# A row gather in a graph attention kernel gets a bound, and edges outside a slot's block get an index past it

## The reference, cut to what matters

```
q, k, v = feats @ Wq.T + bq, feats @ Wk.T + bk, feats @ Wv.T + bv     # 8 heads of 32
sim  = sum(q[dst] * k[src]) * scale          # per edge and head
attn = softmax of sim over the edges of one dst
agg[dst] += attn * v[src]
x = x + agg @ Wo.T + bo
```

## Time and profile before

| | us |
|---|---|
| median of 3 runs | 6892.29 |
| the profiled execution's own time | 6941.69 |
| its span, first to last instruction | 6939.9 |
| attention loop in it | about 3812 to 6740 |
| gathers `kv<-kvt,sI` (L1249) | 1760 of mean 1.008 |

### The profile page before, as it was taken

How to read it: one execution, slowest core, us unless ns; L and a number is a source line. 1 busy time by engine, 2 the same in 40 slices (tenths; PEclk the granted TensorE clock), 3 DMA queues, 4 the chain that set the end, 5 groups by cost and what they waited for, 6 DMA issues and landing times. The chain is left out here.

```text
span 6939.9 us, 112013 instructions
## 1 busy us (share of the span) xinstructions
PE 4544.0 (65%) x19717; PEld 2978.0 (43%) x16197; DVE 4539.5 (65%) x12295; ACT 3970.3 (57%) x14482; POOL 4648.7 (67%) x3716
## 2 busy tenths in 40 slices
PE   1356666666666666664886677777777777777777
PEld 1244444444444545553553333334333333434335
DVE  4565555555555666663554777777777777777766
ACT  0665555555555555552332577777777767777761
POOL 1478888888888888887554566666666666666630
PEclk6677777777777777776998888888888888888889
DMA  8767777777777777777874566666666666676756
GB/s 303 196 103 107 106 106 105 104 107 106 108 107 106 106 110 108 109 109 167 274 260 136 173 188 192 192 190 195 194 192 195 200 200 197 201 206 201 204 151 194
DMA packets 644159, 1129.71 MB, mean 163 GB/s; under 512 B 74529, under 2 KB 466795, under 8 KB 643445
## 3 DMA queue, kind: packets, MB, share of 16 engines
q0 software_dynamic: 367600, 678.97, 50.2%
q1 hardware_dynamic: 223985, 273.78, 12.1%
q10 hardware_dynamic: 51860, 169.74, 7.3%
HBM read 929.80 MB, written 451.51 MB: 199 GB/s over the span
## 5 line engine op out<-in xcount | busy, mean ns | idle before, releaser
L701 POOL DMA_INDIRECT sums<-mtw,posIw x1563 | 2492.0, 1594 | 599.5 <-issue 404.5
L1249 POOL DMA_INDIRECT kv<-kvt,sI x1760 | 1774.2, 1008 | 1027.4 <-ACT room L1631 596.1
L1631 ACT ACTIVATE room<-kv,pp 128x33 f32<-128x33 f32 x8800 | 1932.3, 308 | 107.2 <-issue 101.8
L734 PE MATMUL ps<-h,wf 128*128 x3320 | 1220.8, 522 | 310.0 <-DVE mtw L825 237.3
L1551 PE MATMUL ps<-room,Of 128*128 128x264 f32 x3520 | 1130.8, 459 | 372.2 <-DVE acc L1734 189.0
L718 PE MATMUL ps<-Mw,Oh 128*128 128x128 f32 x3320 | 672.6, 368 | 918.6 <-DVE Oh L852 918.6
L825 DVE SCALAR_TENSOR_TENSOR mtw<-mtw,cont,ps 128x256 f32 x1660 | 794.1, 478 | 620.2 <-SPq L690 459.9
L718 PEld LDWEIGHTS ps<-Mw,Oh 128*128 128x128 f32 x3320 | 631.7, 274 | 1035.3 <-DVE Oh L852 1004.4
L734 PEld LDWEIGHTS ps<-h,wf 128*128 128x128 f32 x3320 | 816.9, 263 | 590.1 <-issue 451.4
L1551 PEld LDWEIGHTS ps<-room,Of 128*128 128x128 f32 x3520 | 707.6, 219 | 659.6 <-issue 278.6
L799 ACT COPY wf<-ps 128x512 f32<-128x512 f32 x415 | 242.4, 584 | 1234.4 <-PE ps L718 902.9
(11 more groups left out here) (224 smaller groups left out, 4796.5 us busy)
## 6 DMA issues: line engine op xcount, KB each, us to landing
qb<-qt SPq DMA_DIRECT2D x880, 192.0 KB
accd<-acc SPq DMA_DIRECT2D x880, 132.0 KB
ints<-srows ACTq DMA_DIRECT2D x205, 512.0 KB
OT<-drows SPq DMA_DIRECT2D x110, 512.0 KB
sums<-zero ACTq DMA_DIRECT2D x72, 704.0 KB
part<-sums SPq DMA_DIRECT2D x56, 896.0 KB
kv<-kvt,sI POOLq DMA_INDIRECT x1760
kvt<-kvo SPq DMA_DIRECT2D x98, 260.0 KB
```

The source lines that it names most:

```text
L701: e.indirect_dma_start(sums[t % NS], bass.IndirectOffsetOnAxis(ap=posI[:, t % NP:t % NP + 1], axis=0), mt[:, t % NM, :], None, compute_op= ...
L734: m = e.matmul(psum[2 + q % 4][:, j % 2 * D:j % 2 * D + D], lhsT=BT[:, g % 3, j % 4, :], rhs=h[:, bass.ds(own[j % 4], 1), :].rearrange("p ...
L1249: e.indirect_dma_start(kv[:, s % NK, :], None, kvt, bass.IndirectOffsetOnAxis(ap=sI[:, s:s + 1], axis=0)).then_inc(kvs.sem(s), 16)
L1631: e.activation(pv[:, s % NV, h * 33:h * 33 + 33], kv[:, s % NK, D + h * 33:D + h * 33 + 33], ACT.Copy, scale=pp[:, w % 2, h, s % W2:s % W2 ...
```

## The change

`gather` gets a bound, `NB * P - 1` = 12543, the last row of the table, and an index above it is no error: that row is not fetched. In the preparation block DVE works out which edges lie outside their slot's block, `(dl2 - 63.5)² > 4096`, for all slots from the 128th on, and adds 65536 to their index, except on partition 0, whose row is always fetched. The first 128 slots keep their indices, and with them each of the 44 ring buffers is filled once in full; a row that is not fetched leaves there what an earlier slot brought.

```diff
             e.indirect_dma_start(kv[:, s % NK, :], None, kvt, bass.IndirectOffsetOnAxis(
-                ap=sI[:, s:s + 1], axis=0)).then_inc(kvs.sem(s), 16)
+                ap=sI[:, s:s + 1], axis=0), bounds_check=NB * P - 1, oob_is_err=False).then_inc(kvs.sem(s), 16)
...
+            far = sb(stack, "far", [P, R2 - P], BF16)
+            skip = sb(stack, "skip", [P, 1])
...
+                e.memset(skip[:, :], 65536.0).then_inc(S("t_skip"), 1)
+                e.wait_ge(S("t_skip"), 1)
+                e.memset(skip[0:1, :], 0.0).then_inc(S("t_skip"), 1)
                 for c in range(C2):
...
+                e.wait_ge(S("t_column"), 2 * C2)
+                e.tensor_scalar(far[:, :], dl2[:, P:R2], 0.5 - P / 2, None, ALU.add).then_inc(S("t_far"), 1)
+                e.wait_ge(S("t_far"), 1)
+                e.tensor_tensor(far[:, :], far[:, :], far[:, :], ALU.mult).then_inc(S("t_far"), 1)
+                e.wait_ge(S("t_far"), 2)
+                e.tensor_scalar(far[:, :], far[:, :], P * P / 4, None, ALU.is_gt).then_inc(S("t_far"), 1)
+                e.wait_ge(S("t_skip"), 2)
+                e.wait_ge(S("t_far"), 3)
+                e.scalar_tensor_tensor(out=sI[:, P:R2], in0=far[:, :], scalar=skip[:, 0:1], in1=sI[:, P:R2],
+                                       op0=ALU.mult, op1=ALU.add)
```

## The result

The changed kernel takes 6939.9 us (median of four runs, 6933.0 to 6951.5) where the kernel before takes 6893.5 (6885.3 to 6896.2) on the same chip. The ratio is 1.0075 [1.0062, 1.0089], so it is slower by 46 us. The forecast was 6776, faster by 116. The profiled execution of the change is close to its median (6938.8 us, span 6936.9), while that of before lay 49 us above its own. So I compare counts, durations and waits between the two pages, and not their spans.

What follows compares the result with a forecast made beforehand. The loop was taken as bound by waits, long gather runs holding up PE and SP. Rows not fetched -121, bound 0, DVE +4.9: -116 us from 6892.3 gives 6776 us, range 6620 to 7010 (the forecast's own 6640 to 6850).

Steps and rivals of the forecast that it cites:

- A long run of gathers holds up what PE and SP owe to the others: Attention loop: other engines' waits let go 2.3 to 2.5 us after POOL stops; ACT's held-up waits total 457.5 us.
- I take one half: -121 us: Loop gathers: rows not fetched give back 2.5 us at each of 97 crossings, 242 us, of which half arrives.
- first rival: Loop: traffic is not what holds it, so rows not fetched bring nothing; 6897 us, chance 0.19.
- these bytes are of another queue: Loop DMA: argument against the no-change rival, whose 3.77 MB more were hardware-queue traffic, not in the gathers' way.
- four long flushes: Loop, SP: 10.76 us over four flushes during a gather run, held not to agree fully with queues taking turns.
- So no cost: Loop gathers: the bound adds 0 to 0.1 us each, covered by POOL's 5.3 us over per window, 0.33 a gather.
- The rival of the dearer gather: Loop gathers on POOL: the bound lengthens all 1760, deciding from 0.33 us extra; 7150 or 7458 us, chance 0.26.
- DVE's operations, +4.9 us: Preparation block: four added DVE operations and two memsets lie on the path, +4.9 us, bounds +3 to +7.
- The data: Loop: unfetched rows hold another node's k and v, but zero one-hot columns leave sizes and counts the same; no cost.
- The sum: Whole kernel: -121 + 4.9 = -116 us, from a median of 6892.3 to 6776 us.
- if they stay, traffic is not the cause: Loop sign: ACT's waits ahead of `tops` and `lim` should fall from 457.5 to some 340 us.
- the rows are fetched all the same: Sign: queue 0 packets should fall 11% over the loop; if they don't, the rows are still being fetched.

Runs made afterwards that it cites:

- pause_quad: Kernel before plus a POOL memset behind each quad's four gathers, from the twelfth quad on; 6862.1 us, ratio 0.9893, on the chip of 6930 us.
- before: The kernel before, unchanged, in the profile behind the prediction; profiled execution 6941.7 us, median of its timed runs 6893.5.
- skip_all_4: Changed kernel with nearly all rows from the 128th slot on beyond the bound; 6984.6 us, 1.0075 against the kernel before, on the chip of 6935 us.
- bound_only_4: Kernel before with only the bound put on each gather, every row fetched; 6985.7 us, ratio 1.0076, on the chip of 6935 us.
- after_again: The changed kernel, unchanged, timed again beside the kernel before on the chip of 6930 us; 6988.9 us, ratio 1.0084.
- ops_only: Kernel before plus DVE's four operations, no bound, added offset zero; 6350.6 us, ratio 0.9998, on the chip of 6356 us.
- skip_all: Changed kernel with nearly all rows from the 128th slot on beyond the bound; 6527.1 us, 1.0264 against the kernel before, on the chip of 6356 us.
- bound_only: Kernel before with only the bound put on each gather, every row fetched; 6525.5 us, ratio 1.0264, on the chip of 6356 us.
- before_again: The kernel before, unchanged, run for a second profile on the chip of 6356 us; 6350.0 us, ratio 0.9995, span 6343.7.

## Why the prediction was wrong

**"A long run of gathers holds up what PE and SP owe to the others": borne out in part.** `pause_quad` agrees with it by a gain of 68 us against 372.7 us of added work, and in `before`, from 3830 to 6600 us, 80 of ACT's 96 waits over 2 us of this kind end while no gather runs, though gathers fill some six tenths of the loop. The release comes at a median of 1.4 us after the last gather, and not 2.3 to 2.5; the two places that I had read were long ones. It was seen on three chips only: on the three others the same instructions have no such wait.

**"I take one half: -121 us" for rows not fetched: this step failed.** The term is 0. The 2.5 us that I gave back for each crossing went by the quieter queue that missing rows leave, and the hold-up does not hang on what that queue moves: with the share of queue 0 at 2.8% for 55.4% it is the same. What is left is the gathers as such, and an empty one is issued like a full one: as long, and with as many packets. (The working beside it has a slip: 0.77 us of the engines for a gather counts 64 packets. By the earlier trace rows 48.94 MB are 184 gathers, so it is 80 packets and 0.96 us; the forecast took 1.25 and did not use it.) The forecast had this as its first rival, with the right argument in the earlier trace rows (3.77 MB more at no cost), and I gave it 0.19 against 0.47. I set the argument aside because "these bytes are of another queue". With it went what I had cited from the Trainium skill (page "DMA: Bandwidth & Descriptors", section "SWDGE vs HWDGE vs iDMA") on queues taking turns, to which I had opposed four long flushes. `skip_all_4` gives the time that I had drawn from that rule, no change by the rows; that the engines take turns it does not show, since its packets are as many.

**"So no cost" for the bound: this step failed too, and it is what made the sign.** The extra, 0.052 us, is within the 0 to 0.1 that I took. The cover was wrong. I read 26.1 - 20.8 = 5.3 us a window as time that POOL has over, from which an extra of 0.33 us would be paid. (With the mean gather of 1.008 us for the 0.95 it is 4.4 us and 0.28; that does not save the step, for the extra is a fifth of it and was not covered.) As I read it now, that idle time is what a hold-up leaves, at its own moments; between two of them POOL issues back to back, and a longer gather moves all behind it. The runs show how much arrives, not this path. `bound_only_4` has 92 us more of gathers by the medians and is 51 us slower, the first comparison 46, `after_again` 59: about half is absorbed, not all. Where there are no hold-ups nothing is: 182 us of gathers for 170 us of time. The rival of the dearer gather had the right sign and mechanism at a price six times smaller than its threshold; a threshold was the wrong form.

**DVE's operations, +4.9 us: right in size,** 4.2 us in the trace and nothing measurable in `ops_only`. The product was put too high (2.0, measured 1.03) and the int32 combination right (2.0, measured 1.95). **The data: right.** On the chip of 6381 us the change equals its bound alone (6526.8 and 6527.4), so other rows in the buffers do nothing.

**The sum, mended:** 0 for the rows, some 50 for the bound (measured, not derived) and 4 for DVE, against 46 and 59 measured. The listed signs pointed the right way in part: of ACT's waits, "if they stay, traffic is not the cause" is what came, though they rose by 123 us. One sign was misread in advance: that packets of queue 0 must fall unless "the rows are fetched all the same". They did not fall, and the bytes did.

**Open.** What a run of gathers does to the semaphores of PE and to SP's list, why the pause gains, and why three chips show hold-ups and three don't. No experiment touched any of them.

## What to carry to other kernels

In these runs a row that a bound rejects saves its bytes and nothing of the instruction that gathers it, and the bound is paid in every gather. So look first whether anything waits for the bytes. Before you let an engine's idle time cover a cost, add the fixed step between its instructions (here 0.30 us for each gather) and ask what makes the idle time: idle time that a stall elsewhere leaves covers only a part. And a gain found by breaking up a stall is to be timed on more than one chip, for here the same edit gives -1.1% and +6.3%.

## What the runs showed of the hardware that was not expected

- A gather of 128 rows with a bound takes 998 to 1002 ns at the median, without one 946. Nearly all rows in or nearly all out, it is the same.
- Rows beyond the bound leave packets of under 512 bytes in the queue: 177,345 of them in `skip_all` against 74,529 in `bound_only`, with 367,600 packets of queue 0 in both. The difference, 102,816, is 1632·63: of each gather from the 128th on, 63 packets of two rows are emptied, and the one with partition 0's row is not.

```profile
DMA packets 644173, 699.55 MB, mean 107 GB/s; under 512 B 177345, under 2 KB 569611, under 8 KB 643445
...
q0 software_dynamic: 367600, 248.69, 30.7%
```

- The same program runs at 6339 to 6381 us on some chips and 6893 to 6935 on others, 8 to 9% apart. Of 596 us between the spans of `before` and `before_again` 564 lie in the loop, where only the slower sort has waits of ACT that end by a semaphore without an instruction behind it, and register operations of SP that take up to 1.4 us.
- POOL's gathers take up to 2.66 us, for 0.96, while DVE runs 2 us operations on one partition.
